# Memory attention: all output products of a period in one run behind the transposes, instead of half of them ahead of the last score bank

## What is computed

```python
Q = layernorm(hidden, g_state, b_state) @ Wq.T           # 8 heads of 128
K, V = (layernorm(memory) @ Wk.T), (... @ Wv.T)          # 256 memory rows
for _ in range(3):
    scores = einsum('bhsd,hnd->bhsn', xi, K) * beta
    w = entmax15(scores)          # square(clip(x - tau, 0)), tau from the row
    xi = einsum('bhsn,hnd->bhsd', w, V)
out = xi.reshape(B, S, H * hd) @ Wo.T
```

## Time and profile before

| | |
|---|---|
| median of three runs | 1932.98 us |
| the profiled execution | 1936.16 us, its span 1934.4 us |
| TensorE matmul busy | 1525.5 us (79%) |
| VectorE, ScalarE, GpSimd busy | 1323.6, 1067.1, 1087.6 us |
| memory attention, periods 0 to 55 | 1108 to 1798 us of the span |
| mean granted TensorE clock | 0.903 |

### The profile page before, as it was taken

How to read it: one execution, slowest core, us unless ns; L and a number is a source line. 1 busy time by engine, 2 the same in 40 slices (tenths; PEclk the granted TensorE clock), 3 DMA queues, 4 the chain that set the end, 5 groups by cost and what they waited for, 6 DMA issues and landing times. The chain is left out here.

```text
span 1934.4 us, 29569 instructions
## 1 busy us (share of the span) xinstructions
PE 1525.5 (79%) x8324; PEld 997.4 (52%) x8324; DVE 1323.6 (68%) x3522; ACT 1067.1 (55%) x2305; POOL 1087.6 (56%) x1248
## 2 busy tenths in 40 slices
PE   4669999999999844079772787778999988889798
PEld 2313333333333323055661576667788867777566
DVE  4467777777777314724355289999999999984342
ACT  1106666666666721000400269999999999997241
POOL 5301564655546553003202159999999999985343
PEclk9859999999999967579985899899999998999899
DMA  3311010010100001500001000000000010000000
GB/s 132 107 36 32 19 30 21 19 31 17 31 19 18 2 1 64 217 0 1 1 0 48 20 1 1 1 1 1 1 1 1 1 44 1 1 1 1 1 23 22
DMA packets 32322, 46.90 MB, mean 24 GB/s; under 512 B 8376, under 2 KB 26704, under 8 KB 31696
## 3 DMA queue, kind: packets, MB, share of 16 engines
q1 hardware_dynamic: 32208, 45.55, 7.3%
HBM read 34.65 MB, written 10.49 MB: 23 GB/s over the span
## 5 line engine op out<-in xcount | busy, mean ns | idle before, releaser
L1799 POOL TENSOR_SCALAR c_R<-c_Z,c_negtau 128x256 f32<-128x256 f32 x519 | 589.7, 1169 | 86.5 <-DVE c_negtau L1868 56.8
L493 DVE TENSOR_REDUCE a_mpart<-a_nat 128x1 f32<-128x512 f32 (+3 forms) x640 | 377.9, 632 | 124.4 <-PE a_nat L620 78.2
L588 ACT ACTIVATE a_PT<-a_sc 128x512 f32<-128x512 f32 x576 | 316.1, 601 | 257.8 <-PE a_sc L653 255.2
L1756 ACT ACTIVATE c_R<-c_Z,c_negtau 128x256 f32<-128x256 f32 x1017 | 425.1, 514 | 3.2 <-DVE c_negtau L1868 1.6
L1835 DVE BATCH_NORM_STATS2 c_stat<-c_R 128x6 f32<-128x512 f32 x576 | 381.1, 679 | 0.9 <-ACT c_R L1756 0.2
L617 PE MATMUL a_nat<-KS,QS 96*128 96x512 bf16 (+3 forms) x768 | 253.4, 347 | 66.9 <-DVE a_mpart L493 34.3
L1686 PE MATMUL c_z<-mem_G,c_R 128*128 128x256 f32 x1024 | 247.0, 399 | 0.1
L460 POOL TENSOR_SCALAR_AFFINE_SELECT a_PT<-a_PT 128x512 f32<-128x512 f32 x128 | 79.4, 639 | 263.8 <-ACT a_PT L588 263.8
L1686 PEld LDWEIGHTS c_z<-mem_G,c_R 128*128 128x128 f32 x1024 | 206.3, 204 | 32.0 <-ACT c_Z L1744 1.7
L653 PE MATMUL a_sc<-QS,KS 128*128 128x512 bf16 (+3 forms) x768 | 217.4, 329 | 3.4 <-ACT a_PT L588 2.5
L1698 PE MATMUL c_T<-ident,c_R 128*128 128x128 f32 x768 | 117.8, 301 | 92.5 <-ACT c_R L1751 91.9
(11 more groups left out here) (329 smaller groups left out, 2138.4 us busy)
## 6 DMA issues: line engine op xcount, KB each, us to landing
qk_parts<-a_parts SPq DMA_DIRECT2D x4, 1536.0 KB, 5.9
QS<-qk_parts SPq DMA_DIRECT2D x192, 32.0 KB
KS<-qk_parts SPq DMA_DIRECT2D x192, 32.0 KB
X<-in_L_attn_x_dram SPq DMA_DIRECT2D x1, 2048.0 KB, 8.5
ternary<-a_W_T SPq DMA_DIRECT2D x1, 2048.0 KB, 6.3
w_q<-in_L_ffn_wq_dram SPq DMA_DIRECT2D x1, 2048.0 KB, 11.6
w_o<-in_L_ffn_wo_dram SPq DMA_DIRECT2D x1, 2048.0 KB, 21.1
W_T<-ternary SPq DMA_DIRECT2D x1, 2048.0 KB, 9.0
```

Of the source, the lines that this page charges most:

```text
L493: dve.tensor_reduce(mpart[:, b, j:j + cnt, i, k0 // 512], src, AX.X, ALU.max).then_inc(s_max, 1)
L588: act.activation(PT[:, n % 3, c, :], sc[:, u % 3, :], ACT.Exp, scale=SCALE0).then_inc(s_exp, 1)
L1756: act.activation(split(i, h) if r < NR else whole(i, h), Z[:, slot(i), h, :], ACT.Relu, bias=threshold(i, r, h)).then_inc(s_ra[r], 1)
L1799: pool.tensor_scalar(split(i, h) if r < NR else whole(i, h), Z[:, slot(i), h, :], threshold(i, r, h), 0.0, ALU.add, ALU.max).then_inc(s_rp ...
```

## The change

TensorE's order within a period alone is altered. No instruction is added or taken out, and no wait's condition is altered; on the other engines nothing moves.

```diff
             for p in range(FIRST, END):
                 some = outputs.get(p, [])
-                half = len(some) // 2
                 if exists(p):
                     scores(p, (0, 1, 2))
                 if p + 1 in begin:
                     turn(begin.index(p + 1))
-                products(some[:half])
                 if exists(p):
                     scores(p, (3,))
                 if exists(p - LAST):
                     transposes(p - LAST, range(4))
-                products(some[half:])
+                products(some)
```

## The result

The changed kernel took 2000.07 us (median of four runs, 1998.52 to 2000.31) against 1933.19 us: the ratio is 1.0342, 95% interval 1.0324 to 1.036, so 66.9 us slower. The forecast was 1987 us, 54 us slower, with a range of 1963 to 2004. The profiled execution took 2000.31 us with a span of 1998.6 us, 64.2 us more than the one of before.

What follows compares the result with a forecast made beforehand. It took TensorE and ScalarE, waiting for each other once a period, to set the pace. Terms 25.4 + 5.1 + 6.9 + 17 = 54.4 us on the 1932.98 us median gave 1987 us, range 1963 to 2004.

Steps and rivals of the forecast that it cites:

- The ring: TensorE and ScalarE wait on each other every period: 14.58 us, 15.26 in turn periods, against 12.85 and 13.5 before.
- the clock: TensorE's longer wait for the first square lowers its clock: 10 losses of 1.69 us, 17 us; bounds 0 to 34.
- TensorE's half of the ring: From ScalarE's first square until score bank 1 can be copied: grows from 6.99 to 8.72 us.
- Periods 19 to 34, 25.4 us: ScalarE waits at its second copy: 9 periods lose 1.69 us, 7 that end with a `ys` lose 1.46.
- Periods 43 to 46, 5.1 us: Periods 43, 44 and 46 lengthen the way to the next scores, without `ys`: 3 x 1.7 us.
- The drain, 6.9 us: From period 48 on, y complete 3.45 us later, felt at unit 45's transposes, and 3.45 us more at the end.
- the second place: Drain's other 3.45 us: behind the last transposes 64 recorded matmuls follow instead of 48, with TensorE the bound.
- (1): Rival: the ring without clock losses, 37.4 us slower, 1970 us; chance 0.19.
- (2): Rival: the clock falls in every period, 71 us slower, 2004 us; chance 0.07.
- (3): Rival: score banks shift ScalarE once per block of periods, then VectorE and GpSimd set the pace; 12 us, 1945; chance 0.07.
- (5): Rival: no effect, the run of 8 products hides as the halves do, 1933 us; chance 0.03.
- (4): Rival: earlier score bank 3 saves up to 4 us in 16 periods, slow stretches fill up, 1921 us; chance 0.02.

Runs made afterwards that it cites:

- e3: Changed kernel plus 3 dummy products between second and third transpose bank in each period up to 47 that holds products: 1973.4 us, 1.0199 of the kernel before.
- e4: Kernel before, but up to period 47 score bank 3 comes early and the first half of products sits between second and third transpose bank: ratio 0.9997.
- e5: Kernel before, but up to period 47 only a quarter of the products stay ahead of score bank 3, three quarters behind the transposes: ratio 1.0092.
- e2: Kernel before with the new order only in periods 48 to 53, the old one before them: 1942.5 us, ratio 1.0045.
- e7: Kernel before, but in periods 48 to 53 all products go ahead of the transposes; old order before that: ratio 1.000.

## Why the prediction was right, and where it was off

The time came out inside the stated range, near its upper end. The ring was right to tenths; the clock was forecast too small.

**What bounds.** Right. TensorE's half of the ring was put at 8.72 us and ScalarE's at 5.86 and 6.54; the periods without a fall of the clock are 14.57 and 15.26 us, to a hundredth or two. That the tie of the two engines, not a busy share of 98%, sets the pace is shown by e3, e4 and e5.

**Periods 19 to 34, 25.4 us.** Shown: e3, where the clock holds but for one fall, takes 25.9 us more than e4 there (240.70 against 214.75). In periods 20 to 34, which have no fall, it is 24.1 us, where the forecast's share of these 15 is 23.7: 1.70 to 1.74 us in the eight that were put at 1.69, and 1.45 to 1.48 in the seven that were put at 1.46 (22, 24 and so on to 34, each behind a period that ends with a `ys`). **Periods 43 to 46, 5.1 us**: e3 59.8 against e4 53.7 us, by period 1.79, 1.73 and 1.75 us in 43, 44 and 46. The 0.8 us left are in period 45, at whose end the clock of e3 fell (from 1732.8 us); in the changed kernel that period is as long as before, 11.12 us. Nothing was gained ahead of bank 3, as taken.

**The drain, 6.9 us.** The sum is right for new idle time (3.42 more at unit 43 and 3.48 at unit 45, e2), if one leaves out the 0.8 us that come back; the second place is not right: I had put it behind the last transposes, where TensorE has no idle time. It arises at unit 43, where half of a tile's products used to fill the time until ScalarE's parts were done. In the changed kernel itself this share is split: TensorE's wait in period 47 is 2.60 us (0.89 before) and the one at unit 43 2.16 (0.44 before). e7 showed the mistake: the same reasoning forecast a gain that did not come.

**The clock, 17 us: mis-sized.** This term holds some 10 of the 12.5 us by which the sum was short. The price of a fall was right (1.6 to 1.7 us), their number was not. I took 10 in 20 from two precedents, one with a fall and one without, and half of two is a guess; that it was no further off is luck. There were 12 in the 16 periods, two more at periods 43 and 46 (17.85 and 18.63 us against e3's 16.24 and 17.02), and in the drain the clock was 0.50 for 13.7 us, against 6.8 in e4. The turn periods, which wait longer, account for most of it: of the eight among periods 20 to 34, with waits of 2.66 to 2.69 us, seven had a fall, of the seven others, with 2.19 to 2.21 us, four. More precedents would not have given this number: in the kernel before, the five waits of 2.19 to 2.20 us in periods without products (12, 18, 35, 38 and 45) had one fall behind them. What decides behind equal waits stays open. From the profiles the clock cost 20.9 us in the 16 periods and 2.4 in periods 43 to 46; by the medians the whole difference to e3 is 26.7 us. With 27 us in place of 17 the sum is 64, against 66.9 measured, which is within the interval (63 to 70 us).

**The rivals.** (1) without the clock's share is what e3 realises, 1973 us, but the kernel itself lies far from it. (2) with a fall each time, 71 us, was closer to the truth than my forecast: 14 falls in 19 periods. (3) a lag, and (5) no effect, are refuted by the lengths of the periods. (4) faster by an earlier bank 3: e4 has the early bank 3 and gains nothing.

**The signs that I had named.** ScalarE's idle time before copies 25 us and more: 38.6. Wait ahead of the third transposes 2.2 to 2.7 us: 2.19 and 2.69. Clock of 0.85 to 0.95 in the stretch: 0.92. TensorE idle before the transposes of unit 45: 3.48 us.

**The loop nest.** The Trainium skill, "TensorE: Matmul & The Clock Gate", section "Loop structure matters more than you think", puts the clock down to how the loop nest keeps matmuls together. The trace agrees with what it says of long waits: the longer run did not help, and with the wait that gathering it opened, 2.19 to 2.69 us, the clock of the 16 periods went from 1.00 to 0.92.

## What to carry to other kernels

Where two engines with in-order queues wait for each other once a period, add up the two halves from release to release: an instruction between the release and what is owed for it costs its full length in every period, one inside the wait costs nothing. Work that is nobody's dependency (here the output products) belongs into the wait, and it pays there twice, since it also kept TensorE at its full clock here (e4: 1.00); a few dummy matmuls brought back 27 us of 67. To find what an end stretch can gain, count the idle time of its bound engine and its time at the lower clock, not the work behind the last dependency.

## What the runs showed of the hardware

In the changed kernel a wait of TensorE of 2.19 to 2.69 us between two groups of transposes was followed by a clock of 0.50 in 11 of the 15 periods 20 to 34; in period 19, with a wait of 3.44 us, the clock fell within the wait. Waits of 1.33 to 1.83 us in the same place (e5) were followed by no fall in 15 periods, and waits of 0.9 to 1.4 us with 6 recorded matmuls ahead of them (e3) by none in 16. Equal waits did not always have the same outcome: periods 24, 28 and 32 of the changed kernel, with 2.19 to 2.20 us, kept the full clock, and so did period 20 with 2.66; periods 21, 26, 29 and 33, also without a turn, lost it.
